# Two context tiles share each weight as it arrives, and one transposition moves among the last tile's products

## The reference, cut to what matters

```python
k_ctx = (h_ctx_kv @ wk_ctx).reshape(B, T, NUM_KV_HEADS, HEAD_DIM)   # T = 4096, HIDDEN = 512
v_ctx = (h_ctx_kv @ wv_ctx).reshape(B, T, NUM_KV_HEADS, HEAD_DIM)
k_ctx = rms_norm(k_ctx, k_norm_w)
...
k_full = jnp.concatenate([k_ctx, k], axis=1)
v_full = jnp.concatenate([v_ctx, v], axis=1)
...
scores = jnp.einsum('blhd,bmhd->bhlm', q, k_full) * scale + mask
probs = jax.nn.softmax(scores, axis=-1)
out = jnp.einsum('bhlm,bmhd->blhd', probs, v_full)
```

## Time and profile before

| | |
|---|---|
| median of 3 runs | 1041.64 us (1041.24 to 1042.82) |
| the profiled execution | 1041.48 us |
| its span, first to last instruction | 1039.8 us |
| granted TensorE clock | 1.000 |
| PE busy | 1034.3 us, 99% of the span |

### The profile page before, as it was taken

How to read it: one execution, slowest core, us unless ns; L and a number is a source line. 1 busy time by engine, 2 the same in 40 slices (tenths; PEclk the granted TensorE clock), 3 DMA queues, 4 the chain that set the end, 5 groups by cost and what they waited for, 6 DMA issues and landing times.

```text
span 1039.8 us, 15687 instructions
## 1 busy us (share of the span) xinstructions
PE 1034.3 (99%) x5837; PEld 889.7 (86%) x5837; DVE 780.3 (75%) x1674; ACT 610.5 (59%) x1106; POOL 183.2 (18%) x200
## 2 busy tenths in 40 slices
PE   9999999999999999999999999999999999999998
PEld 7888888887888888888888888889887988888887
DVE  6856777649777877777877777877669877777775
ACT  5434343335765556665566665569469566666664
POOL 4544434330000000000000000002201132222221
PEclk9999999999999999999999999999999999999999
DMA  7758675399004130042200431004540486555540
GB/s 278 238 187 285 201 243 192 129 318 318 5 1 169 53 124 1 2 172 82 92 1 1 172 122 56 1 1 184 202 163 1 153 294 223 192 183 188 194 165 21
DMA packets 64299, 145.76 MB, mean 140 GB/s; under 512 B 3904, under 2 KB 42720, under 8 KB 62688
## 3 DMA queue, kind: packets, MB, share of 16 engines
q1 hardware_dynamic: 64224, 144.77, 40.2%
HBM read 108.55 MB, written 36.21 MB: 139 GB/s over the span
## 4 chain that ended last, share of the span: by engine, by line
PE 97%; DVE 2%; ACT 1%; DMA 0%; issue 0%; SPq 0%
PE bank L511 17%; PE bank L577 17%; PE bank L493 12%; PE bank L616 12%; PE bank L593 11%; PE bank L877 9%; PE bank L618 6%; PE bank L879 4%; PE bank L673 2%; PE bank L686 1%; PE bank L520 1%; DVE scores L1033 1%; PE bank L741 1%; PE bank L847 1%; PE bank L545 0%; DMA ctx_raw<-in_ctx 0%
## 5 line engine op out<-in xcount | busy, mean ns | idle before, releaser
L1114 DVE TENSOR_TENSOR pT<-bank,pT 128x512 fp32r<-128x512 f32 x272 | 184.7, 689 | 101.9 <-ACT pT L1575 100.1
L1575 ACT CAST pT<-bank 128x512 fp32r<-128x512 f32 x272 | 156.0, 593 | 141.9 <-PE bank L593 138.8
L616 PE MATMUL bank<-pT,vN 128*128 128x512 f32 (+1 forms) x544 | 225.7, 422 | 0.0
L577 PE MATMUL bank<-kT,qT_hi 128*128 128x512 f32 (+2 forms) x576 | 214.4, 391 | 0.7 <-DVE scores L1033 0.7
L1033 DVE TENSOR_SCALAR_CACHE_REDUCE scores<-bank 128x512 f32<-128x512 f32 x256 | 172.5, 686 | 1.6
L593 PE MATMUL bank<-ident,scores 128*128 128x128 f32 x1072 | 161.3, 272 | 0.1
L1546 ACT ACTIVATE scores<-scores,neg_max 128x1024 f32<-128x1024 f32 (+2 forms) x128 | 154.0, 1203 | 6.2 <-DVE neg_max L1045 6.2
L618 PE MATMUL bank<-pT,vN 128*128 128x256 f32 (+1 forms) x544 | 152.5, 280 | 0.0
L511 PE MATMUL bank<-w_ctx_hi,ctx_hl 128*128 128x512 f32 x512 | 144.6, 394 | 0.2 <-ACT ctx_hl L1455 0.2
L877 PE MATMUL bank<-fT_parts,e_hl 128*128 128x512 f32 x392 | 140.0, 395 | 0.0
L593 PEld LDWEIGHTS bank<-ident,scores 128*128 128x128 f32 x1072 | 127.1, 140 | 11.5 <-DVE pT L1114 0.6
(11 more groups left out here) (236 smaller groups left out, 1596.4 us busy)
## 6 DMA issues: line engine op xcount, KB each, us to landing
e_raw<-in_experts SPq DMA_DIRECT2D x51, 768.0 KB, 4.4
k_spill<-k_stage SPq DMA_DIRECT2D x16, 1024.0 KB, 5.7
v_spill<-v_stage SPq DMA_DIRECT2D x16, 1024.0 KB, 8.2
vN<-v_spill SPq DMA_DIRECT2D x16, 1024.0 KB, 5.5
kT<-k_spill SPq DMA_DIRECT2D x15, 1024.0 KB, 5.1
ctx_raw<-in_ctx SPq DMA_DIRECT2D x15, 512.0 KB, 4.2
w_raw<-in_w_qkv SPq DMA_DIRECT2D x6, 1024.0 KB, 5.0
wo_sb<-in_wo SPq DMA_DIRECT2D x4, 1024.0 KB, 7.9
```

The lines of the kernel that those rows point to most:

```text
L577: done = e.matmul(bank[b][:, 0:n], qT[a][:, h, qt * P:(qt + 1) * P], kT[:, w, lo:lo + n], start=m == 0, stop=m == 2)
L616: e.matmul(halves[:, :, q0:L], vN[:, 0, kt, :], ring[:, :, i * L + q0:(i + 1) * L], start=kt == 0, stop=False)
L1114: e.tensor_tensor(ring[:, 1, :], bank[tb][:, :], ring[:, 0, :], ALU.subtract).then_inc(p_lo, 1)
L1575: e.copy(ring[:, 0, :], bank[tb][:, :]).then_inc(p_hi, 1)
```

## The change

It has four edits. (1) The products of tiles 0 and 1 are made in one list, `FIRST_TWO`: the 12 of tile 0 with k = 0, 1, then the 12 of tile 1 with k = 0, 1, then the 12 of tile 0 with k = 2, 3, then the 12 of tile 1. (2) Slice 0 of the weights comes as two DMAs of 256 KB, with context tile 0 between them; context tile 1 is loaded behind slice 1; ACT splits context tile 1 behind slice 1 too. (3) One of the 12 products of ones ahead of the stage is left out. (4) `turn(30)` stands in front of the last four products of `project(31)` and no longer behind them.

```diff
+FIRST_TWO = tuple((0, *p) for p in FIRST_ORDER[:12]) + tuple((1, k, a, w, j) for a, w in ((0, 0), (0, 1), (1, 0)) for k in range(2) for j in range(2)) + tuple(
+    (i, *p) for i in range(2) for p in FIRST_ORDER[12:])
...
-        out_sent = sem("out_x")
+        out_sent = w_values_in = sem("in_first_values_then_out_x")
...
-                order = FIRST_ORDER if i == 0 else TILE_ORDER
+                order = TILE_ORDER
                 for m, (k, a, w, j) in enumerate(order):
+                    if i == NT - 1 and m == len(order) - 4:
+                        turn(i - 1)
...
+            def project_first_two():
+                for m, (i, k, a, w, j) in enumerate(FIRST_TWO):
+                    pe.wait_ge((ctx_hi, ctx_lo)[a], i + 1)
+                    pe.wait_ge((wc_hi, wc_lo)[w], 2 * k + j + 1)
+                    mine = [n for n, (i_, _, _, _, j_) in enumerate(FIRST_TWO) if (i_, j_) == (i, j)]
+                    done = e.matmul(bank[2 * j + i][:, :], ctx_hl[i][:, a, k, :], w_ctx[w][:, k, j, :], start=m == mine[0], stop=m == mine[-1])
+                    if m in (len(FIRST_TWO) - 13, len(FIRST_TWO) - 1):
+                        done.then_inc(ctx_proj, 1)
...
-            for _ in range(12):
+            for _ in range(11):
                 e.matmul(bank[6][:, 0:P], ones[:, :], ones[:, :], start=True, stop=True)
-            for i in range(NT):
-                project(i)
+            project_first_two()
+            for i in range(1, NT):
+                if i >= 2:
+                    project(i)
...
-                if i >= 1:
+                if 1 <= i < NT - 1:
                     turn(i - 1)
...
             for k in range(KD):
                 act.wait_ge(w_ctx_in[k], 16)
                 for j in range(2):
+                    if k == 0 and j == 1:
+                        act.wait_ge(w_values_in, 16)
                     e.copy(w_ctx[0][:, k, j], w_ctx_raw[:, k, j]).then_inc(wc_hi, 1)
-                    if k == 0 and j == 0:
-                        split_ctx(0)
+                    if k == j < 2:
+                        split_ctx(k)
             for i in range(NT):
-                if i + 1 < NT:
+                if 1 <= i < NT - 1:
                     split_ctx(i + 1)
...
-            e.dma_start(w_ctx_raw[:, 0], t["w_ctx"][:, 0]).then_inc(w_ctx_in[0], 16)
+            e.dma_start(w_ctx_raw[:, 0, 0], t["w_ctx"][:, 0, 0]).then_inc(w_ctx_in[0], 16)
             e.dma_start(ctx_raw[0][:, 0], t["ctx"][:, 0]).then_inc(first_in[0], 16)
+            e.dma_start(w_ctx_raw[:, 0, 1], t["w_ctx"][:, 0, 1]).then_inc(w_values_in, 16)
             for k in range(1, KD):
                 e.dma_start(w_ctx_raw[:, k], t["w_ctx"][:, k]).then_inc(w_ctx_in[k], 16)
-            e.dma_start(ctx_raw[0][:, 1], t["ctx"][:, 1]).then_inc(first_in[1], 16)
+                if k == 1:
+                    e.dma_start(ctx_raw[0][:, 1], t["ctx"][:, 1]).then_inc(first_in[1], 16)
...
-            sp.wait_ge(out_sent, 16 * TT)
+            sp.wait_ge(out_sent, 16 + 16 * TT)
```

## The result

Over ten runs each, the changed kernel took 1044.80 us in the median (1042.55 to 1045.71) against 1042.43 for the kernel before (1041.24 to 1042.92): a ratio of 1.0021, 95% interval 1.0013 to 1.0029, so 2.2 us slower (1.4 to 3.0). The forecast was 1042.4 with a range up to 1043.5. A small slowdown was forecast, and the measured one is three times as large; the profiled execution of the changed kernel took 1044.09 us with a span of 1042.2.

The account below looks back on a forecast made before the run. The prediction took PE, busy for 99% of the span, to bound the kernel. To the median of 1041.64 us it added +1.38 at the start and -0.65 at the stage's end, giving 1042.4 us, range 1040.9 to 1043.5.

Parts of the forecast that it names:

- So the fourth product stays at 7.43: cost and gain 0: At the start, the first product needing slice 1 keeps its time, since 1280 KB up to slice 1 are unchanged: 0.
- if slice 1 lands some 0.5 us later in smaller pieces: Upper bound on the loss at the start: not above about +1.9 us.
- Rival D: At the start, the extra DMA costs a whole transfer, 2.1 us more from the fourth product on: 1044.5 us; 5%.
- The late keys: At the start, tile 0 finishes later, so tile 1's keys are late and PE stalls 1.3 us at `turn(1)`: +1.38 us.
- The hold of DVE's piece behind POOL: At the start, DVE's first `w_hl` piece ends 1.08 us behind POOL's split; +1.38 us with the hold, +0.9 without.
- The end of the stage: Moving `turn(30)` nearly removes PE's 0.73 us wait for an eviction at 251.35 and costs 0.09: -0.65 us.
- Case C: Nothing gained at the stage's end, as PE's wait at 251 us hangs on something else: 1043.1 us; 15%.
- Case B: No late keys at the start, worth -0.1 to 0, with the gain at the end kept: 1040.9 us; 22%.

Follow-up runs that it names:

- experiment 1: The changed kernel again, unaltered, in a second profiled execution: 1045.47 us, ratio 1.0031 to the kernel before.
- experiment 6: The filled kernel: the changed kernel with four products of ones between the third and fourth product; 1043.99 us, ratio 1.0017 to the kernel before.
- Experiment 5: The changed kernel with the products of tiles 0 and 1 one tile after the other again: 1043.13 us, ratio 1.0011 to the kernel before.
- experiment 11: The changed kernel with slice 0 whole and DVE taking tile 1's sums before the rest of tile 0's turned keys: 1042.16 us, 1.0002.
- experiment 16: Kernel before with both context tiles behind whole slice 0, both tiles' slice-0 products first, tile 1's sums earlier, transposition of tile 30 moved: 1041.27 us, 0.9991.

## Why the prediction was wrong

**The step that failed** is "So the fourth product stays at 7.43: cost and gain 0". It rested on the bytes up to slice 1 being the same 1280 KB. They are, and slice 1 still came 1.6 us later than in the profiled execution of before. The one more transfer ahead of it was priced by its bytes and its issue; the step was mis-sized by 1.6 us, and it went straight through, as the fourth product carries all behind it. The experiments put three transfers ahead in place of two against a slice 1 that is ready at 8.1 to 8.5 in place of 6.7 to 7.8. A third of it had been in the bounds ("if slice 1 lands some 0.5 us later in smaller pieces").

**Rival D** had the right place, too high a price and too low a chance: a whole transfer's landing, 2.1 us, at 5%. Measured was 1.6 against the trace of before, and less against its usual runs, where slice 1 is copied up to 7.8. The Trainium skill (DMA: Bandwidth & Descriptors, Anatomy of one DMA — SWDGE (gpsimd) path) gives a fixed cost of about 2.0 us for each DMA issued by GpSimd. As a price of one more DMA of SyncE it is not paid in sequence here, since slice 1 comes 0.3 to 1.8 us later. The Trainium skill (DMA: Bandwidth & Descriptors, Bandwidth) advises to batch transfers to 1 MiB and more; the traces agree in direction, as one more small transfer made the next one late, one of 0.5 KB as well.

**What was not reckoned at all** is the clock. The rows of before show 1.00 in every stretch, the kernel before kept 0.999 or 1.000 in nearly all its runs, and I held the pause in front of the fourth product for free of other cost. With the longer pauses the mean clock fell in six of ten runs and in all six of experiment 1. In its trace PE ran at 1.2 GHz for some 3 us, which cost 1.6 us, and the filled kernel's median is 0.8 to 1.5 lower.

**The late keys** were right in mechanism and size. Counted from the fourth product, every time of the chain came within 0.05 us, the rest of `xnT` was 3.11 late (1.51 forecast and 1.6), and PE's pause at `turn(1)` was 1.25 (26.41 to 27.66; 1.3 forecast). Experiment 5 took the pause away by finishing tile 0 first, experiment 11 halved it by DVE's list alone. The hold of DVE's piece behind POOL was not tried by itself, but the trace bears it out: the first piece of `w_hl`, started at 20.31 beside POOL's split, took 1.69 us and not 1.21, and ended 1.09 behind the split's end, where 1.08 was reckoned.

**The end of the stage** was right: 0.74 in the trace for 0.65, and medians of -0.78 and -0.35 alone, neither clear of no change by itself. Case C falls by the traces, where PE's wait is gone. Case B falls too: the keys were late in every trace with the changed kernel's list.

**The sum over the medians.** Forecast 0.7, measured 2.2 to 2.4. Slice 1 is some 1 us later than in the kernel before's usual runs (8.3 against the mean of 6.75, 7.31 and 7.82), and the clock costs about 1.7 us (the gap between the groups of runs, 1045.2 and 1043.5) in six runs of ten, 1.0: 0.7 + 1.0 + 1.0 = 2.7. That is within the interval, but the terms are rough: the four runs at clock 1.000 lie 1.2 above the mean of the kernel before, where the first two terms ask for 1.7. With the clock kept the time stands near the upper end of the stated range, 1043.5, or just above it (1043.5 in those four runs, 1043.99 in experiment 6); so it took the late slice and the clock together to carry it well out. Part of the gap between forecast and median is also the start: the profiled execution of before, 1041.48, lies 0.7 below the median of 21 of its runs, 1042.23; slice 1 came early in it, which is the likely reason and was not tried. The chances for a result outside the band add up to 0.105 and not to the 0.12 of the prediction; nothing hangs on that.

**Left open:** why a third small transfer thins the stream between 4 and 7 us, whether it is the transfers or their rows that count, and why the clock falls in some runs of a kernel and not in others after the same pause.

## What to carry to other kernels

When loads at the head of a queue are cut or reordered, find the first consumer that needs the next transfer; the new transfer's price is paid there, and its bytes do not tell it, and an earlier first piece is worth nothing if that consumer is not moved. When two accumulations are interleaved, the first one's results come later by all that was put between, and every in-order queue that had that result near its head moves along: follow it to the next wait of the bound engine. And a pause at the start can be filled with real work that needs only what is already there, and where that was done here (experiment 16) the clock was kept too.

## What was not expected of the hardware

- A load of 0.5 KB placed third in SP's queue went with slice 1's copy at 8.15 us, against 6.7 to 7.8 with two transfers ahead, and 221 to 259 GB/s in the stream between 4 and 6 us.
- With a second queue issuing beside SP's, the stream had no such hole (404 to 426 GB/s), and yet slice 0 and context tile 0, which are needed first, came later (first copies at 5.77 and 7.40, not 4.84 and 5.49).
- Behind PE's pauses between 6 and 9 us the granted clock stood at 0.50, which is 1.2 GHz, for about 3 us in one execution of the changed kernel; in another it stayed at 1.00.
